# Small aggregation: tiles and blocks written out, sizes of a tile in one load, a semaphore per step

## The reference

```python
h = (x_flat @ W_gat).reshape(M, HEADS, NUM_EXPERTS)          # 4 heads of 4 numbers
e = leaky_relu(a_src[src] + a_dst[dst], negative_slope=0.2)
ee = jnp.exp(e - segment_max(e, dst)[dst])
alpha = ee / (segment_sum(ee, dst)[dst] + 1e-16)
agg = segment_sum(h[src] * alpha[:, :, None], dst).reshape(M, 16) + b_gat
...
for ei in range(4):
    hh = jax.nn.gelu(x @ W1[ei] + b1[ei], approximate=False)  # 256 -> 512
    out = out + g[..., None] * (hh @ W2[ei] + b2[ei])         # 512 -> 256
```

## Time and profile before

| | before |
|---|---|
| median of 3 runs | 10153.3 us (10152.81 to 10157.51) |
| the profiled execution, its own time | 10115.47 us |
| its span, first to last instruction | 10113.7 us |
| instructions in the span | 55153 |
| busy: PE, PEld | 2297.3 us (23%), 1752.3 us (17%) |
| busy: DVE, ACT, POOL | 5569.8 us (55%), 1113.5 us (11%), 5271.3 us (52%) |
| mean granted clock of TensorE | 0.596 of full speed |
| DMA | 458098 packets, 869.24 MB |

### The profile page before, as it was taken

The page is one execution under the profiler, slowest core; times in us unless marked ns, Lnnn a source line. Parts: engine busy times, 40 slices in busy tenths (PEclk is TensorE's granted clock), DMA queues, the critical chain, the costliest instruction groups (busy, mean ns, idle before and its releaser), DMA issues. The chain is left out here.

```text
span 10113.7 us, 55153 instructions
## 1 busy us (share of the span) xinstructions
PE 2297.3 (23%) x9111; PEld 1752.3 (17%) x9112; DVE 5569.8 (55%) x8728; ACT 1113.5 (11%) x2633; POOL 5271.3 (52%) x5411
## 2 busy tenths in 40 slices
PE   2112000000000001246554512000000000129995
PEld 1111000000000001135443411000000000126663
DVE  8764588887877677423232375465566555521111
ACT  1101000000000001112222201000000000002221
POOL 0025666666766644445555345766666766542221
PEclk6555555555555555578777755555555555559997
DMA  4051333433333353311111253333333333620004
GB/s 142 22 158 54 94 88 89 124 101 98 105 99 98 95 125 59 118 23 33 29 28 28 47 156 99 103 98 98 97 98 102 100 98 98 129 98 30 30 30 117
DMA packets 458098, 869.24 MB, mean 86 GB/s; under 512 B 175135, under 2 KB 294861, under 8 KB 448193
## 3 DMA queue, kind: packets, MB, share of 16 engines
q0 software_dynamic: 239536, 575.99, 22.9%
q1 hardware_dynamic: 167648, 182.04, 6.2%
q10 hardware_dynamic: 50788, 110.02, 3.2%
HBM read 693.35 MB, written 180.71 MB: 86 GB/s over the span
## 5 line engine op out<-in xcount | busy, mean ns | idle before, releaser
L914 POOL DMA_INDIRECT agg_ring<-table,agg_idx x4320 | 4209.3, 974 | 2415.4 <-issue 1305.7
L1049 DVE TENSOR_TENSOR agg_part<-agg_ring,agg_prob 128x2048 f32 x420 | 964.4, 2296 | 483.5 <-issue 405.2
L1085 DVE TENSOR_TENSOR agg_wide<-agg_wide,agg_part 128x2048 f32<-128x2048 f32 x420 | 960.4, 2287 | 14.4
L1797 PE MATMUL dense_tp<-all_ident,dense_xn 128*128 128x128 f32 x100 | 23.9, 426 | 2599.4 <-issue 2572.9
L1419 PE MATMUL agg_hp<-agg_xt,agg_w 128*128 128x256 f32 x1600 | 458.6, 446 | 544.4 <-ACT agg_ht L1389 280.5
L2219 DVE TENSOR_TENSOR experts_h<-experts_sg,experts_hp 128x682 f32<-128x682 f32 x106 | 91.8, 866 | 779.0 <-ACT experts_sg L2202 779.0
L2169 PE MATMUL experts_hp<-mixture_w,experts_xt 128*128 x1696 | 517.5, 457 | 0.6 <-ACT experts_xt L2198 0.6
L1797 PEld LDWEIGHTS dense_tp<-all_ident,dense_xn 128*128 128x128 f32 x100 | 20.3, 228 | 2601.1 <-issue 2573.7
L1419 PEld LDWEIGHTS agg_hp<-agg_xt,agg_w 128*128 128x128 f32 x1600 | 356.9, 227 | 634.4 <-ACT agg_ht L1389 298.0
L2140 POOL DMA_INDIRECT yc<-experts_ysb,experts_list x105 | 103.7, 987 | 684.5 <-DVE experts_ysb L2228 684.5
L1433 PE MATMUL agg_yp<-agg_w,agg_ht 128*128 128x256 f32 x1600 | 398.3, 407 | 267.7 <-remote 208.3
(11 more groups left out here) (420 smaller groups left out, 6535.2 us busy)
## 6 DMA issues: line engine op xcount, KB each, us to landing
agg_ring<-table,agg_idx POOLq DMA_INDIRECT x4320
y<-agg_ysb ACTq DMA_DIRECT2D x25, 1024.0 KB
rank_y<-y SPq DMA_DIRECT2D x10, 2560.0 KB
rank_x<-x SPq DMA_DIRECT2D x30, 640.0 KB
copies<-first_sort_words SPq DMA_DIRECT2D x16, 1024.0 KB, 23.0
copies<-last_sort_words ACTq DMA_DIRECT2D x16, 1024.0 KB
x<-rank_x SPq DMA_DIRECT2D x20, 640.0 KB
agg<-agg_res ACTq DMA_DIRECT2D x98, 128.0 KB
```

Of the source, the lines that this page charges most:

```text
L914: pool.indirect_dma_start(out=self.ring[:, to:to + self.RW], out_offset=None, in_=self.table, in_offset=bass.IndirectOffsetOnAxis(ap=index ...
L1049: return dve.tensor_tensor(to[:, :].rearrange("p (j h c) -> p j h c", j=UNIT, h=H), ring[:, ds(st.at(at_u), UNIT * RW)].rearrange("p (j w) ...
L1085: dve.tensor_tensor(wide[:, :], wide[:, :], part[:, :], ALU.add).then_inc(widened, 1)
```

## The change

It touches `aggregate_small` and `SmallExperts` alone.

- All 49 tiles on DVE and ACT, and all 25 blocks on PE, are written out. The tile's number is a constant, and so are the values of waits that count tiles or blocks. The loops over chunks and units stay.
- At the start DVE puts the four sizes of each tile side by side (`sizes`, four copies), and a tile reads its four by one load, on DVE and on ACT (`sizes_of`).
- Each step of a chunk has a semaphore of its own that counts chunks, so one value, `kk`, serves for all waits.
- `acc` and `den` are cleared once and not for each tile. A tile's first chunk multiplies them by exp of (-1e30 minus its maximum), which is 0.
- In the chunk the sum of weights (`dsum`) comes ahead of the scaling of `den`, there are waits between these steps, and the large reduction stands ahead of the addition to `den`. A tile no longer waits for the end of the tile before (`tile_done`).

The core of the diff:

```diff
+        sizes, sized = s.sb("sizes", [1, 4 * NT], I32), s.sem("sized")
+        def sizes_of(eng, t):
+            why = "the ranking bounds every size of a tile"
+            ng, nk, c0, k0 = nc.values_load_multi_w_load_instructions(sizes[0:1, t * 4:t * 4 + 4], engines=[eng.engine], ...)[1]
+            return nc.s_assert_within(ng, UNIT, CH, skip_runtime_bounds_check_because=why), nk, c0, k0
...
+                dve.memset(acc[:, :], 0.0).then_inc(const, 1)
+                dve.memset(den[:, :], 0.0).then_inc(const, 1)
...
+                for w, first in enumerate((I_NG, I_NK, I_C0, I_K0)):
+                    dve.tensor_copy(of_tile[:, :, w], st.inf[:, first:first + NT]).then_inc(sized, 1)
...
-                    ng, nk, c0, k0 = st.tile(dve, t)
+                    ng, nk, c0, k0 = sizes_of(dve, t)
                     dve.wait_ge(st.ready, st.entries((c0 + ng) >> 3))
-                    dve.wait_ge(tile_done, t + 1)
-                    dve.tensor_copy(er[:, :], ...).then_inc(tstep, 1)
-                    dve.memset(m[:, :], NEG).then_inc(tstep, 1)
-                    dve.memset(acc[:, :], 0.0).then_inc(tstep, 1)
-                    dve.memset(den[:, :], 0.0).then_inc(tstep, 1)
-                    dve.wait_ge(tstep, t * TS + TS)
+                    dve.tensor_copy(er[:, :], ...).then_inc(begun, 1)
+                    dve.memset(m[:, :], NEG).then_inc(begun, 1)
+                    dve.wait_ge(begun, t * 2 + 2)
...
-                        dve.wait_ge(cstep, c + 3)
-                        dve.scalar_tensor_tensor(out=sc3, ...).then_inc(cstep, 1)
-                        dve.wait_ge(cstep, c + 4)
+                        dve.wait_ge(added, kk)
+                        dve.scalar_tensor_tensor(out=sc3, ...).then_inc(leaked, 1)
+                        dve.wait_ge(leaked, kk)
...
-                        dve.tensor_tensor(wt4, ..., ALU.mult).then_inc(cstep, 1)
-                        dve.tensor_tensor(den[:, :], den[:, :], prob[:, SC:SC + H], ALU.mult).then_inc(cstep, 1)
-                        dve.tensor_tensor(acc3, acc3, ..., ALU.mult).then_inc(cstep, 1)
-                        dve.tensor_reduce(dsum[:, :], ..., ALU.add).then_inc(cstep, 1)
-                        dve.wait_ge(cstep, c + 12)
-                        dve.tensor_tensor(den[:, :], den[:, :], dsum[:, :], ALU.add).then_inc(inverted, 1)
-                        dve.tensor_reduce(summed[:, :], ..., ALU.add).then_inc(inverted, 1)
-                        dve.wait_ge(inverted, kk * 3 + t * 2 + 2)
-                        dve.tensor_tensor(acc[:, :], acc[:, :], summed[:, :], ALU.add).then_inc(inverted, 1)
-                        dve.wait_ge(inverted, kk * 3 + t * 2 + 3)
+                        dve.tensor_tensor(wt4, ..., ALU.mult).then_inc(weighed, 1)
+                        dve.tensor_reduce(dsum[:, :], ..., ALU.add).then_inc(totalled, 1)
+                        dve.wait_ge(totalled, kk)
+                        dve.tensor_tensor(den[:, :], den[:, :], prob[:, SC:SC + H], ALU.mult).then_inc(shrunk, 1)
+                        dve.wait_ge(shrunk, kk)
+                        dve.tensor_tensor(acc3, acc3, ..., ALU.mult).then_inc(scaled, 1)
+                        dve.wait_ge(weighed, kk)
+                        dve.tensor_reduce(summed[:, :], ..., ALU.add).then_inc(folded, 1)
+                        dve.wait_ge(scaled, kk)
+                        dve.tensor_tensor(den[:, :], den[:, :], dsum[:, :], ALU.add).then_inc(dens, 1)
+                        dve.wait_ge(folded, kk)
+                        dve.tensor_tensor(acc[:, :], acc[:, :], summed[:, :], ALU.add).then_inc(combined, 1)
...
-                tile(0, None)
-                with dve.Fori(0, NT // 2) as i:
-                    tile(i * 2 + 1, None)
-                    tile(i * 2 + 2, lambda: ffn.vector(dve, i))
+                for t in range(NT):
+                    tile(t)
...
-                with pe.Fori(0, NTP // 2) as b:
+                for b in range(NTP // 2):
                     ffn.tensor(pe, b)
...
-                    nk = act.value_load(st.inf[0:1, ds(t + I_NK, 1)], ...)
-                    k0 = act.value_load(st.inf[0:1, ds(t + I_K0, 1)], ...)
+                    _, nk, _, k0 = sizes_of(act, t)
...
+                for t in range(NT):
+                    tile(t)
+                    ffn.scalar(act, t // 2, t % 2)
+                    store(t)
```

More of the change, by code:

```diff
@@ L1201, in aggregate_small @@
         ffn.allocate(nc, s)
+        def sizes_of(eng, t):
+            why = "the ranking bounds every size of a tile"
+            ng, nk, c0, k0 = nc.values_load_multi_w_load_instructions(sizes[0:1, t * 4:t * 4 + 4], engines=[eng.engine], min_val=0, max_val=cfg.max_slots,
+                                                                      skip_runtime_bounds_check_because=why)[1]
+            return nc.s_assert_within(ng, UNIT, CH, skip_runtime_bounds_check_because=why), nk, c0, k0
         with nc.Block() as block:
@@ L1226, in els, with tile @@
                     return chunk[:, ds(j * RW, UNIT * RW)].rearrange("p (j w) -> p j w", w=RW)[:, :, CW:CW + H]
-                def tile(t, beside):
-                    ng, nk, c0, k0 = st.tile(dve, t)
+                def tile(t):
+                    ng, nk, c0, k0 = sizes_of(dve, t)
                     dve.wait_ge(st.ready, st.entries((c0 + ng) >> 3))
-                    dve.wait_ge(tile_done, t + 1)
-                    dve.tensor_copy(er[:, :], ring[:, ds((c0 % cfg.RS) * RW + CW + H, H)]).then_inc(tstep, 1)
-                    dve.memset(m[:, :], NEG).then_inc(tstep, 1)
-                    dve.memset(acc[:, :], 0.0).then_inc(tstep, 1)
-                    dve.memset(den[:, :], 0.0).then_inc(tstep, 1)
-                    dve.wait_ge(tstep, t * TS + TS)
+                    dve.tensor_copy(er[:, :], ring[:, ds((c0 % cfg.RS) * RW + CW + H, H)]).then_inc(begun, 1)
+                    dve.memset(m[:, :], NEG).then_inc(begun, 1)
+                    dve.wait_ge(begun, t * 2 + 2)
                     dve.sem_inc(st.dve_passed, 1)
@@ new lines, in tile @@
+                        dve.wait_ge(added, kk)
+                        dve.scalar_tensor_tensor(out=sc3, in0=sc3, scalar=0.2, in1=sc3, op0=ALU.mult, op1=ALU.max).then_inc(leaked, 1)
+                        dve.wait_ge(leaked, kk)
+                        dve.tensor_reduce(bm[:, :], sc3.rearrange("p j h -> p h j"), AX.X, ALU.max).then_inc(topped, 1)
+                        dve.wait_ge(topped, kk)
+                        dve.tensor_tensor(mn[:, :], m[:, :], bm[:, :], ALU.max).then_inc(raised, 1)
@@ L1276, in tile @@
[L1276 to L1283 removed]
+                                          prob[:, 0:SC].rearrange("p (j h) -> p j h", h=H).unsqueeze(3).to_broadcast([P, SJ, H, C]), ALU.mult).then_inc(weighed, 1)
@@ L1284, in tile @@
+                        dve.wait_ge(dens, kk)
+                        dve.wait_ge(combined, kk)
+                        dve.sem_inc(st.dve_passed, 1)
+                    if t and t % 2 == 0:
+                        ffn.vector(dve, t // 2 - 1)
+                    dve.tensor_scalar(den[:, :], den[:, :], 1e-16, None, ALU.add).then_inc(floored, 1)
+                    dve.wait_ge(floored, t + 1)
                     dve.reciprocal(den[:, :], den[:, :]).then_inc(inverted, 1)
-                    dve.wait_ge(inverted, d + 2)
@@ L1376, in load @@
     def load(self, act, b):
-        src = self.xt_d[2 * b:2 * b + 2, :, :] if isinstance(b, int) else self.xt_d[ds(b * 2, 2), :, :]
+        src = self.xt_d[2 * b:2 * b + 2, :, :]
         act.dma_start(self.xt[:, :].rearrange("p (u n) -> p u n", u=2), src.rearrange("u p n -> p u n")).then_inc(self.xt_in, 16)
     def scalar(self, act, b, half):
-        if half == 0 and not (isinstance(b, int) and b == 0):
+        if half == 0 and b:
             self.store(act, b - 1)
@@ L1390, in scalar @@
                 last.then_inc(self.gelu, 1)
-        if half == 1 and not isinstance(b, int):
+        if half == 1 and b < NT // 2:
             act.wait_ge(self.xt_used, b + 1)
@@ L1402, in vector @@
         dve.wait_ge(self.y_made, b * 4 + 8)
-        dve.wait_ge(self.y_stored, b * 16)
+        if b:
+            dve.wait_ge(self.y_stored, b * 16)
         for u in range(2):
```

80 lines of the change are left out of this document (33 added, 47 removed).

## The result

The changed kernel takes 10250.6 us (four runs, 10246.4 to 10254.6), the kernel before 10155.4 us (four runs): ratio 1.0088, interval 1.0076 to 1.0100. The forecast was 10091 us and the range ended at 10170.

A forecast was written before the change was run, and what follows sets the result against it. It took ACT's and PE's chain plus late stretches to bound the small aggregation, with POOL near. 38.5 (DVE) + 15 (ACT) + 11 (loops) - 3 (new waits) = 62 us less, 10153 to 10091 us; range 9870 to 10170.

The forecast's parts named there:

- late stretches: Small aggregation: times when PE's signals come late and DVE is slow while POOL gathers; 639 us in all, 26 a pair.
- "remote": Wait whose releaser is no instruction that ended just then; ahead of ACT's GELUs it was to stay 400 to 600 us.
- DVE's loads: Sizes of a tile on DVE: one load for four, 3 us less a tile, 38.5 us of it on the path.
- rival A: Small aggregation: the loops cause the late stretches; written out, POOL sets the pace, 9745 us, or 9949 with half; 20%.
- ACT's load: Sizes of a tile on ACT: one load of four registers for two loads, 0.3 us less a tile, 15 us.
- loops: Tile and block loops written out: branches, register operations and counters go, 4 us on ACT and 7 on PE, 11 us.
- semaphores: A semaphore per step in the chunk: two new waits, 0.2 us a tile, 5 us lost at most, 3 taken.
- clears: Sums not cleared: two memsets of some 70 ns a tile go, worth nothing.
- Rival B: Small aggregation: PE stands still for its written-out code, 150 us lost, 88 us slower, 10241 us; 14%.
- Rival C: Small aggregation: POOL runs on sooner into the next late stretch, so almost no gain is left, 10143 us; 14%.
- POOL's wait: POOL's wait for DVE in the small aggregation, 408 us, was to stay above 250; near 0 would mean rival A.
- the packets: Instruction queues were to move many more packets in this stage in every case; under Rival B PE's issue waits grow too.

The follow-up runs named there:

- a_dve4: The changed kernel with DVE's four single loads of a tile's sizes put back, three loaded numbers held at 0 or above: 9111.7 us, kernel before 9104.1.
- a_peloop_again: The changed kernel with PE's 25 blocks a loop again, loaded numbers held at 0 or above: 10229.8 us, ratio 1.0093 to the kernel before; as a_peloop earlier, 9111.2 us.
- the two controls of group 1: The kernel before and the changed kernel, each with three loaded numbers of a tile held at 0 or above: 10114.9 and 10200.5 us (kernel before 10119.1).
- b_dve1: The kernel before with DVE's one load of four sizes alone, loaded numbers held at 0 or above: first 9111.1 us (ratio 1.0006), repeated 10281.7 us (1.0146).
- the five groups: Sets in which the versions were measured, each on one chip with the kernel before beside it; groups 3 and 5 shared a chip.

## Why the prediction was wrong

**The step that failed** is in the paragraph on the sum: "What takes its place: ACT and PE with the late stretches [...] each us that DVE takes slots earlier is a us less of POOL's waiting, and more of the time is then in POOL's runs. I don't charge for that in the sum". The toll of the late stretches, 26 us a pair, was read off as a constant and carried over. It goes by the length of POOL's runs, and that length is set by DVE. The sum put this term at nothing; it was worth more than all the others: "remote" went from 639 us to 855, and the time came out 95 us longer (10250.6 beside 10155.4) where 62 us less were forecast. The earlier trace rows had a part of it: matmuls done 8 us into POOL's run, by their records, and ACT going on 15 us into it while POOL gathered. What wasn't looked at was the pause of 4.63 us that follows, in which the stretch ends (4899.65).

**DVE's loads:** right in direction, too small: the load of four takes 342 ns, not 950, and the idle time ahead of er fell by 253 us, 5.2 a tile, not 3. The 950 leaned on the load of five, which the paragraph on rival A reads as a sign of late stretches; in a_dve4, which has none, that load's median is 1182 ns too. So the earlier trace rows say nothing against rival A. The worth on the path was forecast at 38.5 us, and ACT's waits at exp did fall, by 52.5 us (74.6 to 22.1). But the same edit is the price: in the kernel before, alone, it costs 146 us.

**ACT's load, loops, semaphores, clears:** ACT's load of four takes 310 ns, where 898 were forecast. PE's loop alone is worth nothing that the runs show (a_peloop_again). For the rest no run tells them apart. In the last pair of tiles, where POOL is done, the sums are 31.4 us after the ones before (5864.3 to 5895.7), 32.4 in the kernel before (5750.1 to 5782.5): 1 us a pair; in the two controls of group 1 they are 31.4 and 31.9 us after, half of that. Forecast were 0.6 for ACT's loads and 0.5 for the loops, less 0.2 for the new waits.

**Rival A** (the loops make the late stretches): no. They are there in written-out code, and not there with loops in b_dve1's first run. **Rival B** gave 10241 us, 10 us from the result, by a mechanism that a_peloop_again refutes: a number that fits is no evidence for its story. **Rival C** named the right mechanism (POOL runs on sooner into the next late stretch) and bounded it at the gain it would eat, 10143 us (its own terms, 15 + 4 - 3, make 10137). It had no such bound: a pause that goes away costs the whole stretch that it would have ended.

**The tests that the prediction set:** "remote" left its 400 to 600 us upwards; POOL's wait stayed over 250 us, and rose; the packets came (29 where the earlier trace rows have 3, and 25 in PE's queue, which had 1) and fed PE in time. The stage was to lose 62 us and gained 99. "Gains any" was the sign of a wrong forecast, and it came.

## What to carry to other kernels

An engine that is "not the bound" may still cut another one's work into pieces, and the pieces may matter more than the work: before speeding it up, look at where the pauses of the engine that it feeds lie, and what ends there. When a trace shows waits for "remote" that end at a time set by one engine's runs (here 1.42 us a gather from their start), pace that engine (here 8 gathers and a wait for their landing, 2.2% faster) before anything else is tuned, and measure on more than one chip: where the waits don't exist, each pause is a loss of 2.1 us. A pause must be long enough for the run before it: here 2.3 us did it after 8 gathers, and 2.4 us after 16 didn't. And of two kernels that differ by 1%, one may only be on the lucky side of a limit: 3 us in 20 here.

## What was not expected of the hardware

In four of the five groups, on three chips, and in the run of the result, signals of PE come late while POOL issues indirect gathers without a pause: ACT waits for them for up to 57 us, until 1.42 us for each gather of the run have passed. Many instructions of DVE's sequencer then take 0.70 us, 1403 of them in the whole of the kernel before. In the second group, on a fourth chip, the stage has no such wait, the four traces have one such instruction together, and the kernel before took 1015 us less than in the first. How much of that is the late stretches' isn't shown for all of the kernel; of a_peloop's 1119 us between the two groups 544 lie in the small aggregation (1650.9 and 1106.4 us). Whether it belongs to the chip or to something else that differed between the groups is open. Every run is profiled, so whether it exists without the profiler is open too; so is the cause.
